# Decoder layer with routed experts, one core: order of the last three expert tiles, and their relu on two engines

## The reference, cut to what matters

```python
scores = xf @ gate_W + gate_b
topk_scores, topk_idx = jax.lax.top_k(scores, 2)
weights = jax.nn.softmax(topk_scores, axis=-1)
def expert(w1, b1, g1, be1, w2, b2, g2, be2):      # one of 4
    h = relu(layernorm(xf @ w1 + b1, g1, be1))
    return layernorm(h @ w2 + b2, g2, be2)
out = xf + sum over the two chosen experts of weight * expert(xf)
```

## Time and profile before

| what | value |
|---|---|
| median of three runs | 1214.87 us (1213.1 to 1216.1) |
| profiled execution, its own time | 1209.59 us |
| its span, first to last instruction | 1207.8 us |
| busy: PE / DVE / ACT / POOL | 96% / 77% / 61% / 38% |
| mean granted TensorE clock | 0.988 of full speed |
| data moved by DMA | 143.90 MB, 119 GB/s in the mean |

### The profile page before, as it was taken

One profiled execution on the slowest core, in us unless ns is written; L12 is line 12 of the kernel. 1 busy time (PEld: TensorE's weight loads), 2 busy tenths in 40 slices (PEclk: granted clock), 3 DMA queues, 4 the chain that ended last, 5 costly groups with the idle time before them and its releaser, 6 DMA issues.

```text
span 1207.8 us, 24523 instructions
## 1 busy us (share of the span) xinstructions
PE 1159.6 (96%) x6041; PEld 978.9 (81%) x6042; DVE 924.9 (77%) x2196; ACT 731.5 (61%) x2114; POOL 457.2 (38%) x410
## 2 busy tenths in 40 slices
PE   6999999999989999999999998989999999999993
PEld 5788888888878888888888877867888888888882
DVE  6888888887766677877868777678777777777774
ACT  5323333233486757767677662567777777777773
POOL 4040000000052314535445164357655555555543
PEclk9999999999999999999999998899999999999998
DMA  8754544444520302133021358885554444444433
GB/s 271 230 160 160 188 176 146 174 156 165 199 84 1 105 10 97 44 107 104 10 97 44 131 131 227 270 221 122 81 88 81 85 79 86 80 85 80 85 64 42
DMA packets 83237, 143.90 MB, mean 119 GB/s; under 512 B 20460, under 2 KB 24752, under 8 KB 82309
## 3 DMA queue, kind: packets, MB, share of 16 engines
q1 hardware_dynamic: 63872, 101.60, 25.8%
q0 software_dynamic: 18464, 39.14, 17.1%
q10 hardware_dynamic: 837, 2.41, 0.6%
HBM read 78.83 MB, written 67.83 MB: 121 GB/s over the span
## 4 chain that ended last, share of the span: by engine, by line
PE 83%; DMA 5%; DVE 4%; issue 3%; ACT 3%; POOL 2%; POOLq 0%; DVEq 0%; SPq 0%; ACTq 0%
PE banks L1097 27%; PE banks L681 21%; PE banks L746 7%; PE banks L891 6%; PE banks L879 5%; DMA out<-rows,scatter_rows 4%; PE banks L848 3%; PE banks L865 3%; PE banks L1109 2%; PE banks L907 2%; PE banks L1125 2%; ACT rows L1310 2%; PE banks L719 1%; PE banks L800 1%; PE banks L765 1%
## 5 line engine op out<-in xcount | busy, mean ns | idle before, releaser
L1097 PE MATMUL banks<-operands 128*128 x1608 | 388.6, 396 | 10.5 <-DVE operands L1570 5.2
L1097 PEld LDWEIGHTS banks<-operands 128*128 128x128 f32 x1608 | 298.1, 189 | 73.6 <-issue 7.4
L681 PE MATMUL banks<-operands 128*128 128x512 f32 (+2 forms) x1224 | 292.6, 394 | 3.5 <-DVE operands L1570 3.5
L681 PEld LDWEIGHTS banks<-operands 128*128 128x128 f32 (+1 forms) x1224 | 225.6, 192 | 47.8 <-DVE operands L1570 3.7
L1570 DVE TENSOR_TENSOR operands<-banks,operands 128x512 fp32r<-128x512 f32 (+3 forms) x328 | 217.7, 682 | 42.5 <-ACT operands L1189 38.8
L1189 ACT ACTIVATE operands<-banks 128x512 fp32r<-128x512 f32 (+3 forms) x328 | 191.7, 608 | 96.7 <-PE banks L879 45.0
L1310 ACT ACTIVATE rows<-banks,score_shift 128x77 f32<-128x77 f32 x512 | 162.7, 374 | 28.0 <-DVE score_shift L1792 27.2
L1189 ACT ACTIVATE operands<-rows 128x512 fp32r<-128x512 f32 (+3 forms) x79 | 55.3, 709 | 163.8 <-DVE rows L1641 138.1
L1495 ACT ACTIVATE banks<-banks,param_cols 128x128 f32<-128x128 f32 x268 | 99.2, 430 | 82.5 <-PE banks L1125 82.5
L2576 POOL DMA_INDIRECT out<-rows,scatter_rows x67 | 106.6, 1591 | 104.2 <-DVE rows L2315 65.1
L1310 ACT ACTIVATION_READ_ACCUMULATOR rows<-banks,score_shift 128x1 f32 x512 | 129.1, 256 | 0.0
(11 more groups left out here) (178 smaller groups left out, 1707.0 us busy)
## 6 DMA issues: line engine op xcount, KB each, us to landing
expert_parts<-operands SPq DMA_DIRECT2D x32, 512.0 KB, 3.0
operands<-expert_parts SPq DMA_DIRECT2D x8, 2048.0 KB, 11.1
rows<-in_x SPq DMA_DIRECT2D x8, 1024.0 KB, 5.4
rows<-in_L_ffn_W SPq DMA_DIRECT2D x32, 256.0 KB, 3.5
x_rows<-rows SPq DMA_DIRECT2D x8, 1024.0 KB, 4.3
rows<-x_rows SPq DMA_DIRECT2D x8, 1024.0 KB, 5.7
xf_rows<-rows SPq DMA_DIRECT2D x32, 256.0 KB, 2.7
out<-rows SPq DMA_DIRECT2D x32, 256.0 KB, 2.5
```

The lines of the kernel that those rows point to most:

```text
L681: last = nc.tensor.matmul(dst, stationary(a, k), moving(b, k), start=(t == 0 and k == 0), stop=(t == len(terms) - 1 and k == n_k - 1))
L1097: last = nc.tensor.matmul(dst, stationary[:, a, k, :], weights[:, w, bass.ds(e, 1), a2, k, :].rearrange("p e f -> p (e f)"), start=False, ...
```

## The change

`after` is 4, 3, 2, 1, 0 for tiles 62 to 66. For the last tiles:

- PE: tile 63's second product takes tile 64's `hidden_in` between its 8 and 4 matmuls. Tile 64: `second_product(64)` with `hidden_in(65)` inside, and only then `first_product(66)`. Tile 65: `second_product(65)` and behind it `hidden_in(66)`. Tile 66: `second_product(66)`.
- For tiles 64 to 66 the upper half of the transposed rows goes to another bank (`ch_back` = `cx_bank[1]`). ACT does relu with scale and bias on two of the four blocks, DVE multiplies and adds on the other two (`hidden_affine`). ACT's hi part becomes two instructions of half the width, of which the one on DVE's half does the relu; DVE's lo part becomes two as well (`max` with 0 and subtract on DVE's half).
- DVE: statistics, moments, eps and `norm_shift` of tile 66 move behind y2 of tile 64. `hidden_affine(66)` comes behind the second norm of tile 65.
- POOL: in tile 65 the first-norm `rstd(66)` moves from the front to behind `add_out(64)`; in the kernel before both powers stood ahead of that scatter.
- ACT: in tile 66 `weighed_be2(65)` moves in front of `hidden(66)`.
- Semaphore counts are adapted.

```diff
--- before.py
+++ after.py
@@ -258,6 +258,9 @@
 
         cx_bank, m1_bank, m2_bank = ([ps[:, i, :] for i in pair] for pair in ((4, 5), (6, 3), (1, 7)))
         ch_bank, wb_bank, tail_bank = (ps[:, i, :] for i in (2, 0, 7))
+
+        ch_back = cx_bank[1]
+
 
 
         (const_ready, prow_in, ptr_done, pcol_ready, ctx_in, wk_in, wv_in, wz_in, wh_in, wg_in, bv_in,
@@ -1121,8 +1124,10 @@
 
                 pe.wait_ge(n1_ready, i + 1)
                 need(pe, hl_ready, i)
+                split = isinstance(i, int) and i >= NSLOT - 3
                 for k in range(KC):
-                    last = nc.tensor.transpose(ch_bank[:, k * P:(k + 1) * P], n1[u][:, k * P:(k + 1) * P], ident[:, :])
+                    bank = ch_back if split and k >= KC // 2 else ch_bank
+                    last = nc.tensor.transpose(bank[:, k * P:(k + 1) * P], n1[u][:, k * P:(k + 1) * P], ident[:, :])
                 last.then_inc(ch_done, 1)
 
             def second_product(i, u, e, between=None):
@@ -1144,7 +1149,7 @@
             def c_tile(n, u, coming, after):
                 i = 2 * n + u
                 early = i if isinstance(i, int) else FRONT
-                if after >= 2:
+                if after >= 3:
                     hidden_in(i, u)
                 if after >= 3:
                     rows_in(n + 1 + u, 1 - u)
@@ -1156,9 +1161,13 @@
                     pe.wait_ge(tail_pos_read, 1)
                     prime(m2_bank[1])
                 experts = coming()
-                if after >= 2:
+                if after >= 3:
                     first_product(i + 2, u, experts[4])
-                second_product(i, u, experts[2], (i + 1, 1 - u) if 1 <= after < 3 else None)
+                second_product(i, u, experts[2], (i + 1, 1 - u) if 2 <= after < 4 else None)
+                if after == 2:
+                    first_product(i + 2, u, experts[4])
+                if after == 1:
+                    hidden_in(i + 1, 1 - u)
                 if early == 0:
                     pe.wait_ge(tail_gate_read, 1)
                     pe.wait_ge(route, NROUTE * last + ROUTE_COUNTED)
@@ -1487,17 +1496,22 @@
                 need(act, v2_ready, i - 1)
                 nc.scalar.activation(m2_bank[u], row_of(b2_rows, e), ACT.Copy).then_inc(m2_filled, 1)
 
-            def hidden(i, e):
+            def hidden(i, e, own=KC):
 
                 act.wait_ge(ch_done, i + 1)
-                for k in range(KC):
+                for k in range(own):
                     at = slice(k * P, (k + 1) * P)
                     nc.scalar.activation(ch_bank[:, at], ch_bank[:, at], ACT.Relu,
                                          scale=pcol[:, bass.ds(e * KC + (ROW_G1 + k), 1)],
                                          bias=pcol[:, bass.ds(e * KC + (ROW_BE1 + k), 1)]).then_inc(relu_done, 1)
                 need(act, m2_done, i)
                 act.wait_ge(relu_done, KC * (i + 1))
-                hi_part(hTc[:, HI].rearrange("p k t -> p (k t)"), ch_bank).then_inc(hh_ready, 1)
+                if own == KC:
+                    hi_part(hTc[:, HI].rearrange("p k t -> p (k t)"), ch_bank).then_inc(hh_ready, 1)
+                else:
+                    hi_part(hTc[:, HI, 0:own].rearrange("p k t -> p (k t)"), ch_bank[:, 0:own * P])
+                    nc.scalar.activation(hTc[:, HI, own:].rearrange("p k t -> p (k t)"), ch_back[:, own * P:],
+                                         ACT.Relu).then_inc(hh_ready, 1)
 
             def weighed_be2(n, u, e):
 
@@ -1522,8 +1536,10 @@
                     hidden(i, experts[2])
                     act.wait_ge(primed, 3 + early)
                 fill_second(i, u, experts[2])
+                if after < 1:
+                    weighed_be2(*((n, 0) if u else (n - 1, 1)), experts[1])
                 if early >= 2:
-                    hidden(i, experts[2])
+                    hidden(i, experts[2], KC if after >= 3 else KC // 2)
                 if early == 0:
                     act.wait_ge(b_t_done, t_num(NCH, "xf3") + 1)
                     for j in range(TPC):
@@ -1533,7 +1549,7 @@
                 if early == 1:
                     route_weights(NCH - 1)
                     act.wait_ge(be2_in, 16)
-                if early >= 1:
+                if early >= 1 and after >= 1:
                     weighed_be2(*((n, 0) if u else (n - 1, 1)), experts[1])
                 if after >= 1:
                     hidden_norm(i + 1, 1 - u)
@@ -2282,19 +2298,34 @@
 
             def norm_shift(i):
 
-                dve.wait_ge(c_rstd, i + 1)
+                dve.wait_ge(c_rstd, i + 1 + (isinstance(i, int) and i == NSLOT - 1))
                 V.scalar_tensor_tensor(c_nm[:, 0:1], c_mv[:, 0, 0:1], -1.0, c_rs[:, 0:1], ALU.mult,
                                        ALU.mult).then_inc(nm_ready, 1)
 
-            def hidden_lo(i):
+            def hidden_affine(i, e):
+
+                dve.wait_ge(ch_done, i + 1)
+                for k in range(KC // 2, KC):
+                    at = slice(k * P, (k + 1) * P)
+                    V.tensor_scalar(ch_back[:, at], ch_back[:, at], pcol[:, bass.ds(e * KC + (ROW_G1 + k), 1)],
+                                    pcol[:, bass.ds(e * KC + (ROW_BE1 + k), 1)], ALU.mult, ALU.add).then_inc(relu_done, 1)
+
+            def hidden_lo(i, split=False):
+
                 dve.wait_ge(hh_ready, i + 1)
-                lo_part(hTc[:, LO].rearrange("p k t -> p (k t)"), ch_bank,
-                        hTc[:, HI].rearrange("p k t -> p (k t)")).then_inc(hl_ready, 1)
+                lo, hi = (hTc[:, a].rearrange("p k t -> p (k t)") for a in (LO, HI))
+                if split:
+                    own = KC // 2 * P
+                    lo_part(lo[:, 0:own], ch_bank[:, 0:own], hi[:, 0:own])
+                    V.scalar_tensor_tensor(lo[:, own:], ch_back[:, own:], 0.0, hi[:, own:].bitcast(F32), ALU.max,
+                                           ALU.subtract).then_inc(hl_ready, 1)
+                else:
+                    lo_part(lo, ch_bank, hi).then_inc(hl_ready, 1)
 
             def out_factor(n, u):
 
                 i = 2 * n + u
-                dve.wait_ge(c_rstd, i + 3 + (isinstance(i, int) and i >= NSLOT - 3))
+                dve.wait_ge(c_rstd, i + 3 + (isinstance(i, int) and i >= NSLOT - 2))
                 dve.wait_ge(slots_in[u], 16 * (n + 1))
                 V.tensor_tensor(c_a[:, 0:1], c_rs[:, 1:2], tile_slots[:, bass.ds(i, 1), 1].bitcast(F32),
                                 ALU.mult).then_inc(scale_ready, 1)
@@ -2318,29 +2349,27 @@
                 i = 2 * n + u
                 last = (n, 0) if u else (n - 1, 1)
                 early = i if isinstance(i, int) else FRONT
-                if after == 1:
-                    add_eps(i, True, False)
                 if early == 1:
                     dve.wait_ge(tail_pos_done, 1)
                     shifted_positions(tail_bank, True).then_inc(tail_pos_read, 1)
                     dve.wait_ge(g2_in, 16)
                 if early >= 1:
                     statistics(i - 1, 1, m2_bank[1 - u], m2_done, c2_stat)
-                    expert = coming()[1]
+                    experts = coming()
                     moments(i - 1, 1, c2_stat, c2_aggr)
-                if after == 1:
-                    norm_shift(i + 1)
                 add_eps(i, after >= 2, early >= 1)
                 if after >= 5:
                     gather_rows(n + 2 + u, 1 - u)
                 if early >= 1:
-                    out_shift(*last, expert)
+                    out_shift(*last, experts[1])
                 if after >= 2:
                     norm_shift(i + 1)
                 if early >= 1:
                     out_factor(*last)
                 route_between(early)
-                hidden_lo(i)
+                if after == 0:
+                    hidden_affine(i, experts[2])
+                hidden_lo(i, split=after < 3)
                 if early == 0:
                     dve.wait_ge(tail_gate_done, 1)
                     biased_scores(tail_bank).then_inc(tail_gate_read, 1)
@@ -2348,11 +2377,18 @@
                     count(NCH - 1)
                 if early >= 1:
                     out_rows(*last)
-                if after >= 2:
+                if after >= 3:
                     statistics(i + 2, 0, m1_bank[u], m1_done, c1_stat)
                     moments(i + 2, 0, c1_stat, c1_aggr)
+                if after == 1:
+                    statistics(i + 1, 0, m1_bank[1 - u], m1_done, c1_stat)
+                    moments(i + 1, 0, c1_stat, c1_aggr)
+                    add_eps(i, True, False)
+                    norm_shift(i + 1)
                 if after >= 3:
                     rows_lo(i + 3, 1 - u)
+                if 2 <= after < 4:
+                    hidden_affine(i + 1, experts[3])
                 route_behind(early)
 
             def route_between(tile):
@@ -2580,7 +2616,7 @@
 
                 pool.wait_ge(c_eps, i + 2)
                 if first:
-                    need(pool, n1_ready, i + 1)
```

(6 more changed lines are left out.)

## The result

The changed kernel is slower: median 1221.46 us (1212.79 to 1224.76, 20 runs) against 1215.93 us of the kernel before in 20 runs beside it; the ratio is 1.0043, with an interval of 1.0028 to 1.0058, or 3.4 to 7.1 us. Its profiled execution took 1221.69 us, 12.1 us more than that of the kernel before.

A forecast was written before the change was run, and what follows sets the result against it. The prediction took the series of scatters, 5.6 us apart, to bound the end; a held power and half clock move the last scatter from 1198.36 to 1203.24, +4.9 us on the 1214.87 median: 1219.8 us, range 1215.2 to 1222.0.

The forecast's parts named there:

- Tiles 63 to 65: PE and scatters: second product of 64 at 1177.83, scatter of 63 at 1181.28, scatter of 64 at 1186.93, 0.20 us earlier.
- shorter idles alone bring nothing while the scatters wait for each other: End of kernel: shortening only PE's idles gains nothing, as one scatter behind another costs 5.6 us.
- DVE's multiply-adds: DVE's two 128-wide relu instructions: 0.28 us each by slope, 0.5 for both; cost nothing, at the upper end 0.1 us.
- The held power: POOL, tile 66: power waits behind the scatter of 64 until 1189.13; last transposes at 1190.39.
- From there to the last product: PE, tile 66: 2.68 us from transposes to last product, 1193.07, plus 0.46 for half clock: 1193.53.
- DVE needs 1.96 us from statistics to the scale, so it is ready for the affine at 1191.3: DVE, tile 66: ready for its share of the relu at 1191.3, when the transposes are.
- Moving `weighed_be2(65)` ahead of ACT's relu costs nothing: ACT, tile 66: the moved instruction takes 0.69 us while PE transposes, so no cost.
- The clock: PE, tile 66: half clock after the idle; transposes +0.46 us, last 12 matmuls 5.47 for 3.02, +2.45.
- the sum: End of kernel: last scatter starts at 1203.24 instead of 1198.36, +4.9 us.
- (a): PE, tile 66: rival, clock doesn't fall; last product takes 3.02 us, +2.5 us, 1217.3; chance 0.22.
- (b): POOL, tile 66: rival, the power isn't held and is done at 1186.85; -0.1 us, 1214.7; chance 0.08.
- (c): PE, last tiles: rival, only the idles count, two 0.6 us shorter; 1.2 us less, 1213.7; chance 0.02.

The follow-up runs named there:

- split_only: Kernel before with the relu divided between ACT and DVE for tiles 65 and 66 alone, old order kept; ratio to the kernel before 0.9997 (0.9979 to 1.0015).
- power_first: Changed kernel with POOL's power of tile 66 moved back ahead of the scatter of 64; ratio to the kernel before 1.0021 (1.0002 to 1.0040).
- no_scatter_63: Changed kernel with the scatter of tile 63 left out, its tile missing in the output; not timed, scatter of 64 at 15.60 us for 16.69 after tile 63's start.
- order_only: Changed kernel with the whole relu on ACT again, the new order kept; ratio to the kernel before 1.0042 (1.0024 to 1.0060).
- after_third: Changed kernel unaltered, profiled a third time, on the same chip as before_again; ratio to the kernel before 1.0048 (1.0029 to 1.0067).
- pe_busy: Changed kernel plus unused matmuls on PE, 13 in front of the last transposes and 8 behind; ratio to the kernel before 1.0017 (0.9997 to 1.0037).
- before_again: Kernel before, unaltered, run again against itself; ratio 1.0003 (0.9982 to 1.0024).
- relu_first: power_first plus, in tile 66 on DVE, the relu's multiply-add ahead of tile 65's scale and y2 of 65 ahead of 66's lo part; ratio 1.0011 (0.9995 to 1.0028).
- relu_first_busy: relu_first plus unused matmuls on PE, 4 in front of the last transposes and 8 behind; ratio to the kernel before 1.0000 (0.9984 to 1.0015).
- split_busy: split_only plus 4 unused matmuls in each of the two PE idles; ratio to the kernel before 0.9993 (0.9974 to 1.0011).

## Why the prediction was right

Forecast +4.9 us (1219.8, 1215.2 to 1222.0); measured +5.5 by the medians, 1221.46, and +3.95 at the end in the first pair of profiles. Direction, place and mechanism were right. That the medians came out so close to the forecast is in part luck: by the profiles the end of the kernel gives 3.4 to 4 us, and where the rest of the 5.5 comes from isn't known (last paragraph). By the steps, with 8.02 us taken off the times of the changed kernel:

- **Tiles 63 to 65.** Second product of 64 at 1177.81 (forecast 1177.83), scatter of 63 at 1181.36 (1181.28), scatter of 64 at 1187.09 (1186.93). It was right, too, that shorter idles alone bring nothing while the scatters wait for each other: split_only shows it. DVE's multiply-adds were mis-sized: 0.74 us for the two, not 0.5, nearer the upper end of the bounds. They stand in the chain ahead of the lo part of 64, behind which tile 65's transposes came 0.2 us late (1179.98 for 1179.75); the first product of 66 covered that.
- **The held power.** Ended at 1189.28 (1189.13), last transposes at 1190.35 (1190.39). power_first and no_scatter_63 show the cause from both sides.
- **From there to the last product**: 1193.96 for 1193.53, 0.43 us late. Here a step was off: "DVE needs 1.96 us from statistics to the scale, so it is ready for the affine at 1191.3". It took 2.49 us (1197.46 to 1199.95), the two multiply-adds behind it 0.74 instead of 0.5, and they ended at 1200.96. ACT's own relu had ended at 1200.77; its hi part waited 0.30 us for DVE and began at 1201.06. The rows of DVE show where the 0.53 us lie, in an idle between statistics and moments:

```profile
1197.46 0.70 DVE L2278 BATCH_NORM_STATS2 moe_stats<-banks 128x6 f32<-128x512 f32 x1
1198.83 0.18 DVE L2282 BATCH_NORM_AGGREGATE moe_mean_var<-moe_stats 128x2 f32<-128x6 f32 x1 [0.67 <-DVE moe_stats L2278]
```

  Between the two stands `coming()`, which reads the packed expert numbers of the pair that tile 66 begins into a register (L390). That read took 0.90 us on DVE's queue here and 0.31 in power_first, where statistics and moments lie 0.14 us apart. ACT's queue makes the same read, 0.84 us for 0.28, and that is its 0.54 us of `issue` before the fill of tile 66. It delayed ACT's relu too, but not beyond DVE's multiply-adds, so "Moving `weighed_be2(65)` ahead of ACT's relu costs nothing" held in this trace. In order_only, where ACT has the whole relu, it didn't: the relu began 0.99 us after the transposes had ended (1195.70 to 1196.69), for 0.24 in the earlier trace rows.
- **The clock.** It fell as forecast. The size was off: the last product took 4.34 us, not 5.47, since the clock came back inside it. That is -1.13 on the +4.88 of the sum. With +0.43 from the step above and -0.24 from a y2 that followed the product in 3.18 instead of 3.42 us (POOL was free for its power, for which DVE's scale had waited 0.19 us before), 3.94 are left, and 3.95 were measured. In after_third, no_scatter_63 and order_only it took 4.76, 4.90 and 5.40.
- **Rivals.** (a), no fall, is what pe_busy makes: 30.81 us, or +2.9 for the forecast +2.5. (b), POOL doesn't hold the power, is wrong by the trace; power_first shows what it would have been worth, but not down to -0.1, since the power of tile 65 is then held in its place. (c) is refuted by split_only. The reason given for (a), that idles of 1.8 us leave the clock alone, is wrong as it stands: it fell behind 1.76 and 1.77 us in before_again and order_only. The reason against it, that 2.29 us don't, is no rule either: in relu_first the clock stayed up behind 2.21 us.

What stays open: the medians differ by 5.2 to 5.8 us (1.0043 and 1.0048 of some 1213), the stretches by 3.4 in the mean (32.1 of three for 28.8 of two profiles). 3.4 us would be a ratio of 1.0028, which is the lower end of the first interval (1.0028) and just outside the second (1.0029), so some 2 us of the loss may lie elsewhere. The start of tile 63 was later in all runs of altered kernels (1172.3 to 1179.2) than in the two of the kernel before. This offset doesn't arise in the loop or behind it: the scatter of tile 19 starts at 909.91 in the changed kernel and at 901.86 before, and from it to the start of tile 63 go 268.5 us in all thirteen profiles. It is there ahead of tile 19, where the instructions are the same. Since split_only, with a start of 1174.02, costs nothing by its ratio, it looks like chance in the executions that were profiled; that isn't shown.

## What to carry to other kernels

Where transfers must follow each other, as these scatters that add, ask first whether their series or the compute sets the end; then idles of the busiest engine can be worth nothing (1 us less gave 0.08). Never queue a small power or shift that others wait for behind a transfer that itself waits for a landing: in program order on one engine the small one inherits the whole wait. And price an idle of TensorE with the clock that may fall in it, since the work behind it then takes up to 1.8 times as long.

## What the runs showed of the hardware

- The length of one idle does not say whether the clock falls. Idles of 1.75 to 1.77 us left it at 1.00 in one profile of the kernel before and brought 0.50 in another and in order_only; 1.03 and 2.21 us with 4 transposes between left it up in relu_first, 1.05 and 2.95 brought the fall in power_first. Nor does it always fall in the idle: in the changed kernel it fell 0.3 us before the transposes, in power_first 1.0, in before_again 1.3 and in order_only the first time 1.5 us after PE had begun its next product. With matmuls in the idles (pe_busy, relu_first_busy, split_busy) it stayed at 1.00 until the last product had ended. The Trainium skill (TensorE: Matmul & The Clock Gate, "Part 1: The HAM clock gate") has activity lift the low clock; the changed kernel agrees, where it came back 2.8 us into the last product.
- A multiply-add of 128x128 on DVE, with two per-partition operands chosen by a register, takes 0.41 us (six of them, 410 to 419 ns), and two take 0.74; the slope between one column and 308 had given 0.28.
- A power that comes behind a scatter on POOL ends 2.2 us after the scatter's start, wherever it followed at once (2.19 in the changed kernel and in no_scatter_63, 2.21 in power_first, 2.20 in the earlier trace rows).
- A scatter of 256 KB that adds took 4.87 us to land in the changed kernel and 4.79 and 4.72 in the earlier trace rows. Plain writes of 256 KB that SyncE issues landed in 2.5 and 2.7 us (medians of 32 each, `out<-rows` and `xf_rows<-rows`, in the kernel before). The Trainium skill (DMA: Bandwidth & Descriptors, "Anatomy of one DMA") gives 2.6 us for that size; the plain writes come near it, the scatters don't, and theirs set the end.
- Reading the packed expert numbers from SBUF into a register (TENSOR_LOAD on L390, 25 times on each of three engines) took 0.27 to 0.34 us on DVE and ACT nearly everywhere, and 0.54 to 0.93 us at some places of the last tiles (0.90 and 0.84 in the changed kernel, 0.91 and 0.85 in pe_busy, 0.72 on DVE in before_again). All the slow ones lay where the bytes of a scatter moved (DMA share 0.6 to 1.0), and those of power_first and relu_first, at a share of 0.00, took 0.28 to 0.31. But PE's read at 1198.4 in the changed kernel took 0.3 us at a share of 0.93, so the cause isn't shown.
